# Cross-attention and ternary feed-forward on one core: output bias joined to the projected values, first context load split, engines' work reordered

## What is computed

```python
q = layernorm(x) @ Wq.T + bq;  k = ctx @ Wk.T + bk;  v = ctx @ Wv.T + bv
scores = (q @ k.T) / 16                       # 2048 x 1601
keep the 32 largest of each row, others -inf
x = x + softmax(scores) @ v @ Wo.T + bo
h = bitlinear(layernorm(x), w1, b1)           # rmsnorm, rows to 8 bit, w1 to -1/0/1 times its mean |w|
x = x + bitlinear(gelu(h), w2, b2)            # 256 -> 1024 -> 256
```

## Time and profile before

| | us |
|---|---|
| median of 3 runs | 285.64 (285.26 to 287.21) |
| profiled execution, its own time | 285.15 |
| its span, first to last instruction | 283.3 |
| around the span | 1.85 |

### The profile page before, as it was taken

One profiled execution on the slowest core, in us unless ns is written; L12 is line 12 of the kernel. 1 busy time (PEld: TensorE's weight loads), 2 busy tenths in 40 slices (PEclk: granted clock), 3 DMA queues, 4 the chain that ended last, 5 costly groups with the idle time before them and its releaser, 6 DMA issues. The chain is left out here.

```text
span 283.3 us, 5382 instructions
## 1 busy us (share of the span) xinstructions
PE 263.7 (93%) x1536; PEld 228.6 (81%) x1536; DVE 232.7 (82%) x984; ACT 215.4 (76%) x323; POOL 167.0 (59%) x235
## 2 busy tenths in 40 slices
PE   7999999898997899999999999999999999988784
PEld 7999998897796688787888888878888888867473
DVE  2663778997978897989798979898889997998894
ACT  2657488366599798969797879887988899738762
POOL 3324608921596759676769666975697549712510
PEclk9999999999999999999999999999999999999999
DMA  6981010005000820033002310132003200510011
GB/s 230 312 321 38 3 37 0 22 1 130 1 22 0 168 39 19 2 70 99 19 3 44 108 37 0 27 108 55 0 6 91 56 3 0 130 37 5 0 37 39
DMA packets 29293, 16.44 MB, mean 58 GB/s; under 512 B 20429, under 2 KB 28174, under 8 KB 29262
## 3 DMA queue, kind: packets, MB, share of 16 engines
q1 hardware_dynamic: 28558, 15.02, 19.6%
q0 software_dynamic: 272, 0.79, 1.1%
q10 hardware_dynamic: 432, 0.26, 0.4%
HBM read 9.77 MB, written 2.10 MB: 42 GB/s over the span
## 5 line engine op out<-in xcount | busy, mean ns | idle before, releaser
L398 PE MATMUL bank<-vo,pT 128*128 128x257 f32 (+1 forms) x416 | 97.4, 381 | 3.9 <-ACT pT L1109 3.9
L398 PEld LDWEIGHTS bank<-vo,pT 128*128 128x128 f32 (+1 forms) x416 | 75.9, 190 | 15.2 <-ACT pT L1109 5.4
L1431 DVE MAX8 cand<-s_sb 128x8 f32<-128x50 f32 (+1 forms) x512 | 59.9, 201 | 1.9 <-ACT s_sb L1060 1.1
L257 PE MATMUL score<-k_high,q_low 128*128 128x400 f32 (+1 forms) x128 | 50.2, 393 | 0.0
L871 POOL TENSOR_TENSOR g<-g,b_bc 128x512 f32<-128x512 f32 x24 | 38.7, 1630 | 18.7 <-ACT g L1133 18.7
L257 PE MATMUL score<-k_low,q_high 128*128 128x400 f32 (+1 forms) x128 | 44.2, 346 | 0.0
L257 PE MATMUL score<-k_high,q_high 128*128 128x400 f32 (+1 forms) x128 | 44.0, 344 | 0.0
L1109 ACT ACTIVATE pT<-bank 128x512 f32<-128x512 f32 x64 | 32.0, 517 | 13.3 <-PE bank L265 13.3
L1060 ACT ACTIVATE s_sb<-score 128x400 f32<-128x400 f32 x64 | 31.2, 502 | 8.1 <-PE score L257 8.1
L265 PE MATMUL bank<-ident,e_all 128*128 128x128 f32 (+1 forms) x208 | 31.0, 275 | 5.1 <-DVEq L1505 3.4
L1466 DVE SCALAR_TENSOR_TENSOR e_all<-s_sb,best,e_all 128x1601 f32<-128x1601 f32 x16 | 33.7, 2106 | 1.6 <-ACT e_all L1101 1.2
(11 more groups left out here) (162 smaller groups left out, 492.5 us busy)
## 6 DMA issues: line engine op xcount, KB each, us to landing
x_in<-in_x SPq DMA_DIRECT2D x16, 128.0 KB, 2.3
w_sb<-in_L_ffn_w SPq DMA_DIRECT2D x2, 1024.0 KB, 12.8
x_res<-in_x SPq DMA_DIRECT2D x16, 128.0 KB, 2.2
out<-o_sb SPq DMA_DIRECT2D x16, 128.0 KB, 2.0
ctx_sb<-in_ctx SPq DMA_DIRECT2D x3, 512.0 KB, 6.4
b_bc<-in_L_ffn_b POOLq DMA_DIRECT2D x1, 512.0 KB, 7.6
w_q<-in_L_xattn_Wq SPq DMA_DIRECT2D x1, 256.0 KB, 3.1
w_k<-in_L_xattn_Wk ACTq DMA_DIRECT2D x1, 256.0 KB, 4.3
```

The source lines that it names most:

```text
L257: ins = pe.matmul(out, a, b, start=(i == 0), stop=(i == len(steps) - 1))
L398: ins = pe.matmul(bank[:, 0:DV], pT[0:n, t % 2, b * P:(b + 1) * P], vo[0:n, b, :], start=(b == 0), stop=(b == SB - 1))
L1431: ins = dve.max(cand[:, t % 2, k:CAND:PIECES], s_sb[:, t % 2, k * PIECE:end])
```

## The change

1. `bo_bc` becomes two copies of 256, so that the joined bias can be added to two blocks of values at once. `join_biases` has one more add. The new `add_value_bias(k)` on POOL adds the joined bias to the values of `vo` (blocks 2k and 2k + 1), seven times in all, and the first `weighted` waits for all seven. Since the weights are divided by their sum, this is the same as adding the bias once at the end.
2. `residual(t)` and its semaphore are gone. `attended(t)` waits for the load of `x_res` itself.
3. The first context load of four blocks becomes two of two blocks. Rows are dealt to partitions within a load, so the columns of the first 512 context rows stand in another order; softmax and the 32 largest don't depend on it.
4. `WARM` goes from 30 to 22, `hold_clock` from 24 to 23.
5. The orders of all five engines are written anew.

The diff, cut to its core:

```diff
+CTX_PARTS = ((0, 2), (2, 4), (4, 8), (8, 12))
-WARM = 30
+WARM = 22
...
-        bo_bc = sb("bo_bc", [P, D])
+        bo_bc = sb("bo_bc", [P, 2, D])
...
                 if t == 0 and q == 0:
-                    for k in range(NCTX):
-                        wait_drained(pe, ("vo", k))
+                    pe.wait_ge(vo_ready, NCTX)
...
-            hold_clock(24)
+            hold_clock(23)
...
-            for k in range((SB - 1) // CTX_PIECE):
-                lo, hi = k * CTX_PIECE, (k + 1) * CTX_PIECE
+            for k, (lo, hi) in enumerate(CTX_PARTS):
                 sp.dma_start(ctx_sb[:, lo:hi, :],
...
-                pool.tensor_tensor(bo_bc[:, :], bo_bc[:, :], bvo_bc[:, :], ALU.add).then_inc(bo_ready, 1)
+                pool.tensor_tensor(bo_bc[:, 1, :], bo_bc[:, 0, :], bvo_bc[:, :], ALU.add).then_inc(bo_ready, 1)
                 pool.wait_ge(bo_ready, 1)
+                pool.tensor_tensor(bo_bc[:, 0, :], bo_bc[:, 0, :], bvo_bc[:, :], ALU.add).then_inc(bo_ready, 1)
+
+            def add_value_bias(k):
+
+                nb = min(2, SB - 2 * k)
+                rows = P if 2 * k + nb < SB else S_LAST
+                part = vo[0:rows, 2 * k:2 * k + nb, 0:D]
+                pool.wait_ge(bo_ready, 2)
+                wait_drained(pool, ("vo", k))
+                pool.tensor_tensor(part, part, bo_bc[0:rows, 0:nb, :], ALU.add).then_inc(vo_ready, 1)
...
-            def residual(t):
-
-                pool.wait_ge(x_res_in[t % 2], (t // 2 + 1) * 16)
-                pool.tensor_tensor(x_res[:, t % 2, :], x_res[:, t % 2, :], bo_bc[:, :], ALU.add).then_inc(xb_ready, 1)
...
-                dve.wait_ge(xb_ready, t + 1)
+                dve.wait_ge(x_res_in[u], (t // 2 + 1) * 16)
```

More of the change, by code:

```diff
@@ L268, in turn_context @@
             def turn_context(k):
-                pe.wait_ge(ctx_in[2 * k // CTX_PIECE], 16)
+                pe.wait_ge(ctx_in[sum(hi <= 2 * k for _, hi in CTX_PARTS)], 16)
                 blocks = []
@@ L1232, in _ @@
             take_values(3)
-            sum_weights(1, w2_sb)
             take_values(4)
@@ L1326, in _ @@
             take_weights(13, 3)
-            quantise_2(10)
             copy_scores(15, 0)
-            lower_2(10)
             copy_scores(15, 1)
             copy_scores(15, 2)
+            quantise_2(10)
+            lower_2(10)
             copy_scores(15, 3)
-            take_weights(14, 0)
             quantise_2(11)
             lower_2(11)
+            take_weights(14, 0)
             take_weights(14, 1)
@@ L1711, in _ @@
                     best_8(2 * r + 1, 0)
+                    next_8(2 * r + 1, 1)
+                if live(r - 3):
+                    output(2 * r - 5)
+                if live(r):
+                    next_8(2 * r + 1, 2)
                 if live(r + 2):
@@ L1740, in _ @@
                     count(2 * r + 2)
-                if live(r - 2):
-                    output(2 * r - 4)
+                if live(r - 1):
+                    gelu_max(2 * r - 1)
                 if live(r + 1):
                     weigh(2 * r + 2)
-            largest_count(12)
-            centre(10)
-            release(12)
-            attended(11)
+                    largest_count(2 * r + 2)
+                if live(r):
+                    centre(2 * r)
+                if live(r + 1):
+                    release(2 * r + 2)
+                if live(r):
+                    attended(2 * r + 1)
             moments(11)
-            output(7)
             centre(11)
@@ L1758, in _ @@
             next_8(13, 1)
+            output(7)
             next_8(13, 2)
@@ L1772, in _ @@
             candidates(14, 3)
-            gelu_max(11)
+            output(8)
             best_8(14, 0)
             next_8(14, 1)
+            gelu_max(11)
             next_8(14, 2)
@@ L1779, in _ @@
             weigh(14)
+            candidates(15, 0)
+            attended(13)
             largest_count(14)
-            output(8)
+            moments(13)
+            candidates(15, 1)
+            centre(13)
             release(14)
-            attended(13)
-            moments(13)
-            output(9)
-            centre(13)
-            candidates(15, 0)
-            candidates(15, 1)
             candidates(15, 2)
             candidates(15, 3)
+            output(9)
             best_8(15, 0)
```

380 lines of the change are left out of this document (173 added, 207 removed).

## The result

The changed kernel takes 284.36 us (median of 10 runs, 283.12 to 285.06) against 285.64 (10 runs): a ratio of 0.9936 with a 95% interval of 0.992 to 0.9952. It is faster by 0.6%, 1.3 us, where 8 us were forecast. Its profiled execution took 284.93 us, with a span of 282.3 us (before: 283.3).

The account below looks back on a forecast made before the run. The prediction took PE's own list to bound the kernel. Start, adds, steady rounds, end and the last 20 us summed as 285.15 − 0.9 + 0 − 6.0 − 0.7 + 0.2 = 277.75, say 277.7 us; range 274.5 to 284.

Parts of the forecast that it names:

- What bounds the kernel: Whole span: PE, busy for 93%, is bound by its own list; gains lie in its gaps and the filler transposes.
- (a): Steady rounds: `scores(2r + 1, 3)` ahead of `turn_weights(2r, 0)`, 1.1 to 1.2 us, removes all of PE's waits for `p_ready`.
- (b): Steady rounds: PE's wait for ACT's copy of odd weights goes; about 0.2 of 0.58 us comes back a little later.
- (c): Steady rounds: `squares` behind `exp_all` makes `row_scales_2` later, scale at 152.4; `quantise_2` waits 1.0 us, PE does not wait.
- Rival 3: Steady rounds: `row_scales_2` holds ACT; scale x us after 152.4 makes PE wait x − 1, 288.5 at x = 2.8; chance 0.09.
- Rival 1: Steady rounds: PE's waits only move, start and end gains alone remain, 283.7 us; chance 0.22 together with rival 4.
- rival 4: Joined bias and order change nothing on the path: Rival 1 without the end, 284.2 us; chance 0.22 together with it.
- `residual` is gone: Steady rounds: 16 POOL adds go, DVE's chain gets about 1.2 us shorter, PE's 0.31 us wait for `y1` goes.
- The seven adds: POOL before the first `weighted`: they end at 41.3, PE wants them at 42.9, so cost 0; bounds 0 and +2.0 us.
- Rival 2: Before the first `weighted`: adds are slow beside DVE's two-input instructions, +2.0 us, 279.7 in all; chance 0.09.
- The start: Before `fold_queries`: 8 fewer warm-up transposes and an earlier context load give −0.9 us, bounds 0 and −1.0.
- The end: Last tiles: one `keep_residual` instead of two `residual` ahead of `quantise_1(6, 1)` gives −0.7 us, bounds 0 and −1.1.

Follow-up runs that it names:

- after_normalise_first: The changed kernel with both `normalise` halves of a pair ahead of `row_scales_2` on POOL: 277.89 us, ratio 0.9713 to the kernel before.
- normalise_and_squares_first: after_normalise_first with, on ACT, `squares` of the odd tile also ahead of `exp_all`: 278.45 us, ratio 0.9733 to the kernel before.
- residual_ahead_of_squares: after_normalise_first with the bias joined once again and two `residual` adds a round on POOL, ahead of `row_scales_2`: 280.98 us.
- release_14_earlier: after_normalise_first with `release(14)` on DVE moved ahead of `candidates(15, 1)` and `centre(13)`: 278.57 us, ratio 0.9735 to the kernel before.
- before_bias_joined: The kernel before with the bias change alone (seven adds to `vo`, no `residual`), old orders, loads and warm-up: 287.49 us, ratio 1.0076.
- after_squares_first: The changed kernel with, on ACT, `squares` of the odd tile ahead of `exp_all` again: 281.20 us, ratio 0.9824 to the kernel before.
- after_warm30: The changed kernel with 30 warm-up transposes instead of 22: 285.34 us, ratio 0.9973 to the kernel before.

## Why the prediction was wrong, point by point

- **What bounds the kernel** (PE's own list, with its gaps as all that can be won): right. Both kernels have PE 93% busy, and the large differences between the experiments came through waits of PE. The 1.3 us of the whole change did not: PE's idle time is 283.3 − 263.7 = 19.6 us before and 282.3 − 262.5 = 19.8 after.
- **(a) and (b), the waits for `p_ready` and for the copies**: right, size included. 3.9 fell to 0.6 and `p_ready` went from the rounds. What comes back at the bank, 0.4 us a round in after_normalise_first, was forecast as 0.2.
- **(c), `squares` behind `exp_all`: this is the step that failed.** It followed `row_scales_2` to its reader on ACT, found a wait of about 1 us there that PE would not feel, and stopped. The same block has a second thing behind it, on its own engine: both halves of `normalise`, 2.54 us, which the shown order of POOL had moved there, and behind them `turn_queries` on PE. By the step's own numbers, scale ready at 152.4, this gives 152.4 + 0.3 + 2.5 = 155.2 for `xn`, against a PE that should arrive earlier than the 155.45 of before by all it gains. That was no room at all, and the step had it as nothing.
- **The size of `row_scales_2` was off too, and its start the other way.** I took 2.66 us to its scale from the earlier trace rows. It took 181.79 − 177.57 = 4.22, since its first step, 0.19 us before, now starts under DVE's `weigh` (177.24 to 179.12) and ends with it: 177.57 + 1.60 = 179.17. The Trainium skill (SBUF — State Buffer, "SBUF: two separate sides") says that a VectorE instruction with two SBUF inputs and a GpSimd instruction that reads SBUF exclude each other for the whole of the one that started first; the trace agrees with it here. The cost of a small instruction is then that of the large one in its way, 1.4 us. In the round compared with the earlier trace rows it began at 148.28, not at 149.7, so that its scale came at 152.5, as forecast: the two errors cancel, by luck. What failed is the reader that was left out. Timeline of POOL there:

```profile
148.28 1.59 POOL L885 TENSOR_SCALAR row<-g_ssq 128x2 f32<-128x2 f32 x1 [5.59 <-ACT g_sq L1146]
```
- **Rival 3 had the right block and the wrong reader.** ACT waits 2.52 us a round for `row_scales_2` where 1.0 was forecast, so its x was 1.5, below the 2.8 that it wanted, and PE felt none of it: in normalise_and_squares_first nothing more is won. The rival named `gelu_max`; that `squares` would be the last of the two came true by 0.16 us only.
- **Rival 1, "the waits only move"**, gave 283.7 and rival 4 284.2, the nearest to the result, and in the steady part moved waits are what happened. But their reason, that tight places let one wait take the place of another, is not it: it is one wait, and it was avoidable. Both also counted 0.9 for the start, which did not come, so that 284.2 is so near by luck.
- **`residual` is gone**: that DVE's chain gets shorter is right in the new order (2.97 us of wait a round when the pass is put back), and of no effect in the old one. I had priced it by the 0.31 us of PE's wait for `y1`; it carries 3.1 to 10.6 us, by where the pass would stand.
- **The seven adds**: 0, as forecast. There is no wait for `vo`, and `count` of tile 0 took 0.48 us. From the start of `fold_queries` to the first weighted sum it is 44.38 − 7.12 = 37.26 us in after_normalise_first and the same 43.16 − 5.90 in residual_ahead_of_squares, which has no adds. Rival 2 did not come here, but it did in the old order, through DVE and not through `vo`.
- **The start, −0.9: failed.** The term took 0.16 us per transpose, the mean of the row. That mean mixes long and short ones: a record is 0.43 us long in the first part of the old row and 0.27 in the last. In the changed kernel's row all 22 are long, at 0.23 us from one to the next, so that the row is as long as before and the fold starts 0.5 us later instead of 0.9 earlier.
- **The end, −0.7**: the wait of 1.07 for `y` is gone, but 1.85 us for `release(14)` came near it (243.06), and release_14_earlier shows that taking this away brings nothing. From the last turn of `xn` to the end 1.5 us were won, so the −0.7 may well have come; no run takes it by itself.
- **The range** reached to 284.0 and the result is 284.36. With the 7.9 us of waits for `xn` in it, the sum would have been 277.7 + 7.9 = 285.6.

## What to carry to other kernels

When a block that waits is moved on an in-order engine, write down everything that is queued behind it on that same engine, with its reader and the time that reader wants it, before looking at who reads the block itself. A wait with under 0.1 us of slack does not show among the waits, so look at when the inputs of PE's next turns were ready, and not only at what it waited for. A part of a change can be worth nothing in the old order (the residual pass taken out, 0.9997) and up to 10.6 us in the new one, so undo it there as well as doing it alone.

## What the runs showed of the hardware

The warm-up transposes, all of one shape, start 0.16 us apart on average in one kernel's row (30 in 4.86 us) and 0.21 in another's (30 in 6.38 us, before_bias_joined), with PE's program up to there the same, and the fold starts at 6.65 against 8.17:

```profile
1.52 6.38 PE L460 MATMUL score<-ident 128*128 128x128 f32 x30 [1.52 <-POOL ident L741]
```

The granted clock reads 1.00 in this stretch in both. The moment from which the transposes run closer together differs from one profiled execution to the next; with 22 of them the row took from 4.11 (residual_ahead_of_squares) to 4.96 us. The Trainium skill (TensorE: Matmul & The Clock Gate, Part 1) says that the number of slow matmuls at the start of one kernel varies between runs; one profile for each kernel agrees with that and can't prove it. A start-up edit is to be judged by medians: two profiled starts of the same list differ here by up to 1.5 us.

POOL and DVE held each other up in both directions: a POOL step of 0.19 us took 1.60 behind `weigh`, and a DVE `count` of 0.48 us took 1.40 beside an add that POOL began 0.03 us after it. By the recorded starts this second pair does not follow the rule that the one that starts first has the way; the add's record is 1.09 us long where its neighbour at 37.04 has 1.29, so its start may be recorded late, which no run shows. Nor is a step held that starts together with `weigh`: in after_squares_first the second step of `row_scales_2` began 0.01 us behind it (175.89 against 175.88) and took 0.70 as always, and the third, begun at 176.68, took 1.15 instead of 0.20 and ended with `weigh`, 177.83 against 177.77.

The granted clock can fall to 0.50 inside a run that is at 1.00 everywhere else: in after_warm30 from about 97.5 to 101, after PE had waited 2.10 us. The same wait, 2.11 us, was followed by no fall in the changed kernel's profiled execution.
